# Cross-attention with grouped queries on one core: output weights split during the query projection, reciprocals taken inside attention, last denominator summed on TensorE

## The chip, the cores and the metric

The kernel runs on one core of a Trainium2 chip. The core has TensorE (PE), VectorE (DVE), ScalarE (ACT), GpSimd (POOL) and SyncE (SP), each with its own instruction stream, and 16 DMA engines. The streams are joined only by semaphores that the kernel sets and waits on by hand. The metric is the device time of one execution in microseconds, as the median of several runs.

## The reference, cut to what matters

```python
B, L, S, H, NH, KVH, HD = 4, 1024, 1601, 1024, 32, 8, 32
q, k, v = x @ Wq + bq, ctx @ Wk + bk, ctx @ Wv + bv          # 8 key heads, 4 query heads each
scores = einsum('bkgld,bksd->bkgls', q, k) / sqrt(HD) + mask
attn = softmax(scores, axis=-1)
out = einsum('bkgls,bksd->bkgld', attn, v) @ Wo + bo
x = out + hidden
y = (x - mean(x)) * rsqrt(var(x) + EPS) * gamma + beta
```

All arrays are float32. The mask is all zeros in these inputs; the kernel looks at it and takes a branch without it.

## The kernel before

To keep float32 accuracy in TensorE's fast format, an operand is split in two parts: `hi`, a rounded copy that ACT writes, and `lo`, the rest, which DVE writes as operand minus `hi`. A product is then three matmuls: hi by hi, lo by hi, hi by lo. The program is three blocks one after the other. A block begins only when every engine has ended its stream of the block before, waits for transfers included.

**`project`** makes k and v from 13 chunks of 512 context rows, then q from 8 chunks (NXC) of 512 rows of x. One query chunk is eight groups `g` of 24 matmuls. ACT copies a group's sum to `o_hi` (L308), DVE makes `full` and `o_lo` (L362, L367), POOL stores both (L405). In the last chunk nothing of a next chunk lies beside. SP loads rows and, in query chunks, four mask tiles per chunk into `landing` (L189), which DVE looks through (L346) at odd `g`. POOL waits for its own last store before its stream ends.

**`attend`** runs 64 steps (NSTEP), one for each key head and 512 queries; four steps are a QUAD. The order of TensorE's work in a step is one written string, ORDER: L is a logit tile (13 key tiles by 4 heads), S half a row of scores for the maxima (reduced on DVE, L880), M a product with v of the weights of one key tile, T a transpose of the maxima, P the denominators of the step before. ACT takes the exponents (L933). POOL adds the weight tiles of nine key tiles into `sum_pool` with eight adds (L660); the key tiles of REST = (2, 5, 8, 11) are added to tile 2 by accumulating DMAs that POOL issues (L671), and `merge` (L678) adds that sum to `sum_pool` by one more. P multiplies `sum_pool` with ones (`sum_heads`, L799: four heads, eight instructions in the profile), ACT copies the result to `denom_sb` (L950), SP stores it to `d_dram` (L598). The denominators of step 63 come after everything: the rest of the adds, the merge, `denominators`, the copy, the store. SP's stream in one iteration n of a step is: `load_step` for three steps ahead (q, k, v of 1.5 MB), `store` of the product, `store_sums`, `shift` of the maxima. Near its start it loads 128 of the 1024 rows of Wo, `wo_early`. In the last three steps there is nothing to load.

**`output`** first loads all denominators in two portions (L1048, step 0 to 7 and the rest), takes reciprocals on DVE (L1145), stores them (L1044), and reads them back spread over 32 partitions for each head (`r_in`, L1058); `a_in` holds the products (L1052). DVE multiplies (L1154), ACT and DVE split the result (L1120, L1158). Meanwhile ACT issues the loads of the other seven slices of Wo (L1115) and, after its first `a_hi`, splits them:

```python
            split_hi(0, 0)
            split_weights(range(EARLY, KVH))
            split_hi(0, 1)
```

TensorE (L1103) waits in the first group for each slice of `wo_lo` (L1150), and then runs 1536 matmuls in 16 blocks of 96. Per tile of 128 rows DVE adds x + bo (POOL, L1205), takes the statistics, and normalises; POOL adds beta (L1212) and stores.

Of the kernel before, what the change touches and what calls it, by code (L numbers as in the profile page):

```python
# [20 lines left out]
F32 = mybir.dt.float32  # L21
# [26 lines left out]
EARLY = 1  # L48
# [5 lines left out]
def xattn_program(nc, x, ctx_kv, mask, wq, bq, wk, bk, wv, bv, wo, bo, gamma, beta, out):  # L54
# [10 lines left out]
    r_dram = nc.dram_tensor("reciprocals", [NSTEP, G, LQ], F32, kind="Internal").ap()  # L65

    with ExitStack() as whole:
        ident = whole.enter_context(nc.sbuf_tensor("ident", [P, P], F32))
        mask_size = whole.enter_context(nc.sbuf_tensor("mask_size", [P, MT], F32))
        project(nc, x_flat, ctx_flat, mask_flat, wq, bq, wk, bk, wv, bv, q_dram, k_dram, v_dram, ident, mask_size)  # L70

        wo_early = whole.enter_context(nc.sbuf_tensor("wo_early", [P, EARLY, H], F32))
        attend(nc, mask_flat, q_dram, k_dram, v_dram, a_dram, d_dram, ident, mask_size, wo, wo_early)
        output(nc, x_flat, wo, wo_early, bo, gamma, beta, a_dram, d_dram, r_dram, out_flat)


def project(nc, x_flat, ctx_flat, mask_flat, wq, bq, wk, bk, wv, bv, q_dram, k_dram, v_dram, ident, mask_size):
# [42 lines left out]
    with ExitStack() as held:  # L120
# [11 lines left out]
        bv_row = sb("bv_row", [P, KV])  # L132
# [6 lines left out]
        v_out = [sb(f"v_out{i}", [P, KV]) for i in range(2)]  # L139
# [12 lines left out]
        W_RUNS = (range(KVW), range(KVW, KVW + 3), range(KVW + 3, KVW + 6), range(KVW + 6, len(w_pieces)))  # L152
        w_in = [sem(f"w_in{i}") for i in range(LAND)]
# [23 lines left out]
        def _(sp):  # L177
# [12 lines left out]

            def step(kind, c, par):

                turns = kind == "ctx" and isinstance(c, int) and c == NCC - 1
                following = ("x", 0) if turns else (kind, c + 1)
                for half in range(2):
# [13 lines left out]
            sp.dma_start(bv_row[:], bv.partition_broadcast(P)).then_inc(bias_in, 16)  # L209
            all_chunks(sp, step)  # L210

# [56 lines left out]
        def _(act):  # L268
# [16 lines left out]

            def split_hi(u, t, par):
# [3 lines left out]
            def step(kind, c, par):  # L290
# [4 lines left out]
                for g, beside in enumerate(BESIDE[kind]):  # L295
# [4 lines left out]
                    if kind == "ctx" and isinstance(c, int) and g == 2:  # L300
                        split_weights_hi(W_RUNS[c - NCC + 4])
                    if kind == "x" or g < KG:
# [23 lines left out]
        def _(dve):  # L326
# [14 lines left out]

            def look_through(c, j):
# [6 lines left out]
            def step(kind, c, par):  # L349

                u, n0 = chunk(kind, c), sums(kind, c)
                for g, beside in enumerate(BESIDE[kind]):
# [3 lines left out]
                    if kind == "ctx" and isinstance(c, int) and g == 2:  # L356
                        split_weights_lo(W_RUNS[c - NCC + 4])
                    acc = summed[bank(kind, par, g)]
# [9 lines left out]
                    else:  # L368
# [3 lines left out]
                        nc.vector.tensor_tensor(v_out[j % 2][:], acc[:, 0:KV], bv_row[:], ALU.add).then_inc(sum_read, 1)  # L372
# [13 lines left out]
        def _(pool):  # L386
# [8 lines left out]
            def step(kind, c, par):  # L395
# [12 lines left out]
                if kind == "ctx":  # L408
                    for j in range(XC // P):
                        pool.wait_ge(sum_read, sums(kind, c) + (KG + j + 1 + 4))  # L410
                        pool.dma_start(v_dram[bass.ds(start(c) + j * P, P), :], v_out[j % 2][:]).then_inc(v_stored, 16)  # L411
# [6 lines left out]
def attend(nc, mask_flat, q_dram, k_dram, v_dram, a_dram, d_dram, ident, mask_size, wo, wo_early):  # L418
# [7 lines left out]
    BASES = 2  # L426
    NPOOL = len(POOL) - 1
# [48 lines left out]
    with ExitStack() as held:  # L476
# [7 lines left out]
        q_sb = [sb(f"q_sb{i}", [SHIFT, G, LQ], F32R) for i in range(QB)]  # L484

        k_sb = [sb(f"k_sb{i}", [SHIFT, S], F32R) for i in range(QB)]
# [10 lines left out]
        denom_sb = [sb(f"denom_sb{i}", [P, LQ]) for i in range(2)]  # L497
# [35 lines left out]
        wo_in = sem("wo_early_in")  # L533
        sync_seen = sem("sync_seen")
        mixed_stored = [sem(f"mixed_stored{i}") for i in range(2)]
        denom_stored = [sem(f"denom_stored{i}") for i in range(2)]
# [6 lines left out]
        def _(sp):  # L543
# [50 lines left out]
            def store_sums(step, par):  # L594
# [3 lines left out]
                sp.dma_start(d_dram[bass.ds(step, 1)].rearrange("a h l -> (a h) l"), denom_sb[par][0:P:HD, :]).then_inc(denom_stored[par], 16)  # L598

            def batch(b, first=False, last=False):  # L600
                for lq in range(NB):
                    for n in range(KVH):
# [8 lines left out]
                        elif not last:  # L611
                            load_step(b + 1, 0, ahead % KVH)
# [632 lines left out]
```

## Time and profile before

| | us |
|---|---|
| median of 3 runs | 3967.89 (3964.56 to 3978.52) |
| the profiled execution, its own time | 3971.06 |
| its span | 3969.4 |
| PE busy | 3806.3 (96%) |
| PE weight loads busy | 2407.2 (61%) |
| DVE busy | 2502.5 (63%) |
| ACT busy | 2037.3 (51%) |
| POOL busy | 2905.9 (73%), nine tenths and more in nearly all slices of attention |

Mean granted clock of TensorE 0.963 of full speed. Busy time counts only instructions that compute. In the rows, times count from the start of the span; `[x <-y]` is idle time of the engine before the row and what ended it. PEclk is the granted clock, DMA the mean busy share of 16 engines. `PEld` is a weight load, `SPq`, `POOLq` a sequencer that issues.

### The profile page before, as it was taken

The numbers are of one execution on the slowest core, as the hardware profiler recorded it, in microseconds if no ns is written. First come the engines' busy times: TensorE is split into PE (matmuls) and PEld (weight loads), VectorE is DVE, ScalarE is ACT, GpSimd is POOL, SyncE is SP. The second block draws the span as 40 slices with busy tenths as digits, with TensorE's granted clock in tenths as the row PEclk, the third lists the DMA queues.
The fourth block names the chain that finished last, engine by engine and source line by source line (L and its number), as shares of the span: only waits on it lengthen the run. The fifth ranks groups of instructions, "written<-read, shape, count | busy, mean of one in ns | idle before, by whom it ended". The sixth has DMA issues, their size and how long they took to land. (4 is left out here: it accounts for less than half of the span.)

```text
span 3969.4 us, 66216 instructions
## 1 busy us (share of the span) xinstructions
PE 3806.3 (96%) x20274; PEld 2407.2 (61%) x20274; DVE 2502.5 (63%) x2890; ACT 2037.3 (51%) x3854; POOL 2905.9 (73%) x1108
## 2 busy tenths in 40 slices
PE   8999999799999999999999999999999999967998
PEld 7998888555555555555555555555555555525887
DVE  3334444477767676676777767677676767715666
ACT  2222111056666666666666666666666666641110
POOL 1111111169989899999999999999999999973664
PEclk9999999789999999999999999999999999977999
DMA  5445555547667666766766766666766766655664
GB/s 176 143 139 184 205 200 183 140 94 154 147 132 153 139 141 135 154 137 136 153 144 143 154 135 145 148 145 140 154 137 143 153 135 145 127 139 177 191 196 132
DMA packets 286020, 598.38 MB, mean 151 GB/s; under 512 B 126848, under 2 KB 164096, under 8 KB 252928
## 3 DMA queue, kind: packets, MB, share of 16 engines
q0 software_dynamic: 58368, 339.25, 38.2%
q1 hardware_dynamic: 223056, 245.09, 23.1%
q10 hardware_dynamic: 4272, 9.96, 0.7%
q8 instruction: 175, 2.87, 0.3%
q14 instruction: 149, 1.22, 0.1%
HBM read 236.11 MB, written 88.60 MB: 82 GB/s over the span
## 5 line engine op out<-in xcount | busy, mean ns | idle before, releaser
L880 DVE TENSOR_REDUCE half_max<-score 128x1 f32<-128x800 f32 (+1 forms) x2048 | 1895.0, 986 | 799.5 <-PE score L744 797.3
L933 ACT ACTIVATE weights<-logit 128x512 f32<-128x512 f32 (+1 forms) x3328 | 1736.2, 603 | 855.6 <-PE logit L789 831.4
L660 POOL TENSOR_TENSOR sum_pool<-sum_pool,weights 128x2048 f32<-128x2048 f32 (+1 forms) x448 | 2124.8, 4743 | 40.8 <-ACT weights L933 21.4
L789 PE MATMUL logit<-q_sb,k_sb 98*128 98x512 f32 (+1 forms) x3328 | 1207.4, 420 | 39.8 <-issue 37.2
L744 PE MATMUL score<-k_sb,q_sb 96*128 96x400 f32 (+1 forms) x4096 | 1225.8, 382 | 15.4 <-DMA k_sb<-k_parts 10.6
L744 PEld LDWEIGHTS score<-k_sb,q_sb 96*128 96x128 f32 x4096 | 703.0, 195 | 581.3 <-DVE half_max L880 399.2
L799 PE MATMUL mixed<-weights,v_sb 128*32 128x512 f32 x6656 | 825.0, 610 | 0.7 <-ACT weights L933 0.7
L789 PEld LDWEIGHTS logit<-q_sb,k_sb 98*128 98x128 f32 (+1 forms) x3328 | 618.1, 189 | 280.7 <-issue 151.3
L799 PEld LDWEIGHTS mixed<-weights,v_sb 128*32 128x32 f32 x6656 | 178.8, 110 | 402.2 <-ACT weights L933 223.2
L660 POOL TENSOR_TENSOR sum_pool<-weights 128x2048 f32<-128x2048 f32 x64 | 304.3, 4754 | 114.2 <-ACT weights L933 110.3
L405 POOL DMA_DIRECT2D q_parts<-o_hi x64 | 34.5, 540 | 299.1 <-DMA q_parts<-o_lo 141.6
L1103 PE MATMUL acc<-wo_hi,a_hi 128*128 128x512 f32 x512 | 202.5, 395 | 44.6 <-DVE a_lo L1158 37.7
L308 ACT ACTIVATE o_hi<-summed,bq_scaled 128x512 fp32r<-128x512 f32 x64 | 44.1, 689 | 312.6 <-PE summed L228 312.6
L1103 PE MATMUL acc<-wo_hi,a_lo 128*128 128x512 f32 x512 | 201.6, 394 | 0.0
L1103 PE MATMUL acc<-wo_lo,a_hi 128*128 128x512 f32 x512 | 201.4, 393 | 0.0
L362 DVE TENSOR_SCALAR full<-summed,bq_scaled 128x512 f32<-128x512 f32 x64 | 48.1, 751 | 197.8 <-ACT o_hi L308 197.8
L1212 POOL TENSOR_TENSOR total<-total,beta_row 128x1024 f32<-128x1024 f32 x32 | 102.2, 3193 | 95.5 <-DVE total L1179 95.5
L288 ACT CAST t_hi<-turned 128x512 fp32r<-128x512 f32 x168 | 95.3, 584 | 141.1 <-PE turned L223 140.9
L671 POOL DMA_DIRECT2D weights<-weights x192 | 166.6, 868 | 0.0
L1205 POOL TENSOR_TENSOR total<-total,bo_row 128x1024 f32<-128x1024 f32 x32 | 90.6, 2834 | 80.4 <-DMA total<-in_x 80.1
L411 POOL DMA_DIRECT2D v_rows<-v_out x52 | 28.1, 540 | 162.6 <-DMA v_rows<-v_out 103.8
L333 DVE TENSOR_TENSOR t_lo<-turned,t_hi 128x512 fp32r<-128x512 f32 x168 | 113.0, 685 | 41.8 <-ACT t_hi L288 41.6
(80 smaller groups left out, 2654.4 us busy)
## 6 DMA issues: line engine op xcount, KB each, us to landing
weights<-weights POOLq DMA_DIRECT2D x192, 1024.0 KB, 7.5
sum_pool<-weights POOLq DMA_DIRECT2D x64, 1024.0 KB, 7.3
q_sb<-q_parts SPq DMA_DIRECT2D x192, 256.0 KB, 3.9
k_sb<-k_parts SPq DMA_DIRECT2D x192, 200.1 KB, 6.3
rows<-in_ctx SPq DMA_DIRECT2D x26, 1024.0 KB, 5.2
landing<-in_mask_Bx1xSxS_ff SPq DMA_DIRECT2D x32, 800.5 KB, 5.2
rows<-in_x SPq DMA_DIRECT2D x16, 1024.0 KB, 5.3
q_parts<-o_hi POOLq DMA_DIRECT2D x64, 256.0 KB, 2.3
```

The costliest lines, as they stand in the source:

```text
L288: nc.scalar.copy(t_hi[par][:, t, :], turned[t % 2][:]).then_inc(hi_done, 1)
L333: nc.vector.tensor_tensor(t_lo[par][:, t, :], turned[t % 2][:], t_hi[par][:, t, :].bitcast(F32), ALU.subtract).then_inc(lo_done, 1)
L660: nc.gpsimd.tensor_tensor(sum_pool[s % 2][0:w], first[0:w], weights[buffer(s, st)][0:w], ALU.add).then_inc(pool_added, 1)
L671: pool.dma_start(weights[buffer(s, REST[0])][:], weights[buffer(s, st)][:], accum_op=ALU.add).then_inc(rest_added, 16)
L744: last = nc.tensor.matmul(score[j][:, c, 0:w], q_sb[buf][0:STACK, h, lt * P:(lt + 1) * P], k_sb[buf][0:STACK, start:start + w], start=True ...
L789: last = nc.tensor.matmul(bank[0:w, :], k_sb[s][:, keys], q_sb[s][:, h, :], start=True, stop=not masked, skip_group_check=masked)
L799: last = nc.tensor.matmul(out[h * HD:(h + 1) * HD, :], lhs, rhs[0:w, h, :], start=start, stop=stop)
L880: nc.vector.tensor_reduce(half_max[m // NROW % 2][:, k % G, k // G, j:j + 1], score[j][:, :, 0:HALVES[j][2]], mybir.AxisListType.XY, ALU.m ...
L933: nc.scalar.activation(weights[buffer(s, st)][0:w, h, :], logit[u % BANKS][0:w, :], ACT.Exp).then_inc(exp_done, 1)
L1103: last = nc.tensor.matmul(acc[j * NT + t][:, n, :], a[:, k, cols], w[:, k, out_cols], start=(k == 0 and m == 0), stop=(k == KVH - 1 and m ...
L1205: nc.gpsimd.tensor_tensor(total[r][:], total[r][:], bo_row[:], ALU.add).then_inc(resid_done, 1)
L1212: nc.gpsimd.tensor_tensor(total[r][:], total[r][:], beta_row[:], ALU.add).then_inc(final, 1)
```

## The change

1. Wo is split in `project`, during the last two query chunks: SP loads one slice at a time into `wo_raw` (the buffer of `v_out` and `bv_row`), ACT and DVE split it at g = 1, 3, 5, 7 into the buffers of the k and v weights, and SP stores the eight parts of a chunk to `wo_dram` after its fourth split. The block ends when all sixteen are stored. Ten parts are loaded in the last three steps of attention into the q and k buffers that are then free and one spare; six (3 MB) at the start of `output`.
2. In attention SP loads the denominators of the quad before at n % 4 = 1, DVE takes their reciprocals (128 x 64) in the third step of a quad ahead of its maximum k = 8, and SP stores them at n % 4 = 2. `denom_sb` becomes one buffer. `output` does this only for the last quad, after its first two blocks are ready.
3. In step 63 POOL stops after the key tiles below LATE = 10. TensorE sums what is left itself, five `sum_heads` in one bank: key tiles 10, 11, 12, the tile of the REST sum, and `sum_pool`.

```diff
+        wo_raw = sb("v_store", [P, H])
+        WO_AT = (1, 3, 5, 7)
+            def load_wo(c, t):                         # project, SP
+                k = c * 4 + t
+                if k == 0:
+                    for i in range(2):
+                        sp.wait_ge(v_free[i], NCC * (XC // P // 2) + 1)
+                else:
+                    sp.wait_ge(wo_lo_done, k)
+                sp.dma_start(wo_raw[:], wo[k * P:(k + 1) * P]).then_inc(wo_in, 16)
+            def store_wo(c):
+                sp.wait_ge(wo_lo_done, c * 4 + 4)
+                for t in range(4):
+                    for n, part in enumerate((wo_hi, wo_lo)):
+                        sp.dma_start(wo_dram[2 * (c * 4 + t) + n], part[t].bitcast(F32)).then_inc(wo_stored, 16)
                     for j in range(MPC):
+                        if split:
+                            load_wo(c - NXC + 2, j)
                         load_mask(c, j)
+                    if split:
+                        store_wo(c - NXC + 2)
             all_chunks(sp, step)
+            sp.wait_ge(wo_stored, 16 * 2 * KVH)
+            def split_wo_hi(c, t):                     # ACT, ahead of o_hi of g in WO_AT
+                act.wait_ge(wo_in, (c * 4 + t) * 16 + 16)
+                if c > 0:
+                    act.wait_ge(wo_stored, 16 * KVH)
+                nc.scalar.copy(wo_hi[t], wo_raw[:]).then_inc(wo_hi_done, 1)
+            def split_wo_lo(c, t):                     # DVE, ahead of full of g in WO_AT
+                dve.wait_ge(wo_hi_done, c * 4 + t + 1)
+                nc.vector.tensor_tensor(wo_lo[t], wo_raw[:], wo_hi[t].bitcast(F32), ALU.subtract).then_inc(wo_lo_done, 1)
...
+            def load_wo(j):                            # attend, SP, in iterations 61 to 63
+                sp.wait_ge(logit_done, LOGITS0 + (NSTEP - SLOTS + j) * (ST * G))
+                slots = wo_dram[j * SLOTS:(j + 1) * SLOTS]
+                sp.dma_start(qk_store[j][:, 0:SLOTS * H]..., slots.rearrange("t p n -> p t n")).then_inc(wo_in, 16)
+                if j == 0:
+                    sp.dma_start(wo_spare[:].bitcast(F32), wo_dram[3 * SLOTS]).then_inc(wo_in, 16)
-                            store_sums(step - 1, (n - 1) % 2)
+                            store_sums(step - 1)
+                        if n % QUAD == 1 and not (first and lq == 0 and n < QUAD):
+                            load_sums(quad - 1)
                         if not (final and n == KVH - 1):
                             shift(step + 1, (n + 1) % QB)
+                        if n % QUAD == 2 and not (first and lq == 0 and n < QUAD):
+                            store_reciprocals(quad - 1)
-            sp.dma_start(wo_early[:], wo[0:EARLY * P]...).then_inc(wo_in, 16)
+                    if last and POOL[n + 1] >= LATE:   # POOL, sums()
+                        break
-            merge(NSTEP - 1, QUAD - 1)
+            def last_denominators():                   # PE, after the last product
+                bank, s = logit[SUMS % BANKS], QUAD - 1
+                pe.wait_ge(exp_done, NSTEP * ST * G)
+                for st in range(LATE, ST):
+                    w = min(P, S - st * P)
+                    sum_heads(bank, ones[0:w, :], weights[buffer(s, st)], w, st == LATE, False)
+                pe.wait_ge(rest_added, ...)            # accumulating DMAs of tiles 5 and 8
+                sum_heads(bank, ones[:], weights[buffer(s, REST[0])], P, False, False)
+                pe.wait_ge(pool_added, ...)            # POOL's six adds
+                sum_heads(bank, ones[:], sum_pool[s % 2], P, False, True).then_inc(denom_done, 1)
+            def invert(quad):                          # DVE, at s == 2, k == 8
+                dve.wait_ge(dens_in, quad * 16 + 16)
+                nc.vector.reciprocal(dens[:], dens[:]).then_inc(dens_recip, 1)
...
             for j in range(2):                         # output, SP
                 load_weighted(0, j)
-            store_reciprocals(0)
-            for j in range(2):
                 load_reciprocals(0, j)
+                if j == 0:
+                    sp.dma_start(wo_late[:].bitcast(F32), wo_dram[len(wo_slots):2 * KVH]...).then_inc(wo_late_in, 16)
+            sp.dma_start(dens[:], last_steps(d_dram)).then_inc(dens_in, 16)
             for row, src in ((bo_row, bo), (gamma_row, gamma), (beta_row, beta)):
                 sp.dma_start(row[:], src.partition_broadcast(P)).then_inc(rows_in, 16)
             for j in range(2):
                 load_x(0, j, first=True)
-            store_reciprocals(1)
+            sp.wait_ge(dens_recip, 1)
+            sp.dma_start(last_steps(r_dram), dens[:]).then_inc(dens_out, 16)
+            sp.wait_ge(dens_out, 16)
-                                if t == 0 and n == 0:
-                                    pe.wait_ge(w_lo_done, k + 1)
+                                if t == 0 and n == 0 and k == len(wo_slots) // 2:
+                                    pe.wait_ge(wo_late_in, 16)
             split_hi(0, 0)                             # ACT; DVE likewise
-            split_weights(range(EARLY, KVH))
             split_hi(0, 1)
```

## Rows read from the trace of the kernel before

**Rows 1.** The chain that ended last: start, us, what.
```profile
3559.56 0.35 SPq L1048
3563.17 14.88 DMA reciprocals<-dens
3579.44 7.62 DMA r_in<-reciprocals
3587.08 2.30 DVE a_in L1154
3589.41 1.91 ACT a_hi L1120
3591.34 2.29 DVE a_lo L1158
3593.63 16.63 DVE wo_lo L1150 x7
3610.30 346.34 PE acc L1103 x1515
```
**Rows 2.** Timeline of PE, end of attention: start, us, instructions, idle before.
```profile
3519.49 1.90 PE L799 MATMUL mixed<-weights,v_sb 128*32 128x512 f32 x16
...
3535.73 1.06 PE L799 MATMUL mixed<-weights,v_sb 65*32 65x512 f32 x8 [0.68 <-ACT weights L933]
3554.25 1.94 PE L799 MATMUL logit<-sum_pool,ones 128*32 128x512 f32 x8 [17.45 <-DMA sum_pool<-weights]
3593.90 0.76 PE L1103 MATMUL acc<-wo_hi,a_hi 128*128 128x512 f32 x1 [37.72 <-DVE a_lo L1158]
```
**Rows 3.** Timeline of POOL in step 63.
```profile
3529.64 0.85 POOL L671 DMA_DIRECT2D weights<-weights  x1
3530.24 9.47 POOL L660 TENSOR_TENSOR sum_pool<-sum_pool,weights 128x2048 f32<-128x2048 f32 x2
...
3547.17 0.87 POOL L678 DMA_DIRECT2D sum_pool<-weights  x1 [2.11 <-DMA weights<-weights]
```
**Rows 4.** Timeline of SP, last store of attention.
```profile
3556.94 0.58 SPq L598 DMA_DIRECT2D denominators<-denom_sb  x1
```
**Rows 5.** Windows of 5 us: busy per engine (instructions), PEclk, DMA share, GB/s.
```profile
3570.00:3575.00 5.00, 0.00 (x0) 0.00 (x0) 2.39 (x2) 0.00 (x0) 0.00 (x0) 0.50 1.04 402
...
3580.00:3585.00 5.00, 0.00 (x0) 0.00 (x0) 0.00 (x0) 0.00 (x0) 0.00 (x0) 0.50 0.96 193
...
3610.00:3615.00 5.00, 4.70 (x11) 3.73 (x12) 3.03 (x3) 2.50 (x2) 0.00 (x0) 0.50 0.26 50
3615.00:3620.00 5.00, 5.00 (x21) 4.05 (x21) 2.23 (x2) 0.69 (x1) 0.00 (x0) 0.91 0.00 0
```
**Rows 6.** Timelines of DVE and POOL, end of the query projection.
```profile
743.77 0.69 DVE L367 TENSOR_TENSOR o_lo<-full,o_hi 128x512 fp32r<-128x512 f32 x1
...
750.88 0.54 POOL L405 DMA_DIRECT2D q_parts<-o_lo  x1
755.15 0.12 POOL L644 MEMSET ones<- 128x32 f32 x1 [3.73 <-POOLq L120]
```
**Rows 7.** DMA issues: queue, count, size, median us to landing; last row `a_in` after 3555.
```profile
out<-total POOLq DMA_DIRECT2D x32, 512.0 KB, 2.9
...
q_parts<-o_hi POOLq DMA_DIRECT2D x64, 256.0 KB, 2.3
...
DMA to landing us min/median/max: 5.4/6.7/16.9
```
**Rows 8.** Lines and tiles of DVE: ns min/median/max, or busy us and mean ns.
```profile
L884 DVE TENSOR_REDUCE row_max<-half_max x64: 185/186/189, 807.0 to 3481.9; 128x16 f32<-128x32 f32 x64
...
L1145 DVE RECIPROCAL dens<-dens 128x128 f32<-128x128 f32 x1 | 1.0, 954 | 74.6 <-DMA dens<-denominators 74.6
...
L1150 DVE TENSOR_TENSOR wo_lo<-wo_late,wo_hi x7: 1218/3371/3403, 3593.5 to 3606.9; 128x1024 fp32r<-128x1024 f32 x7
```
**Rows 9.** Timeline of DVE in step 31 or so of attention.
```profile
2110.19 4.59 DVE L880 TENSOR_REDUCE half_max<-score 128x1 f32<-128x804 f32 x5 [1.60 <-PE score L744]
```

More of the change, by code:

```diff
@@ L194, in step @@
                 following = ("x", 0) if turns else (kind, c + 1)
+                split = kind == "x" and isinstance(c, int)
                 for half in range(2):
@@ L481, in sem @@
             return held.enter_context(nc.semaphore(name))
-        q_sb = [sb(f"q_sb{i}", [SHIFT, G, LQ], F32R) for i in range(QB)]
-        k_sb = [sb(f"k_sb{i}", [SHIFT, S], F32R) for i in range(QB)]
+        stores = qk_store + [sb("qk_store3", [P, G * LQ + S], F32R)]
+        q_sb = [store[0:SHIFT, 0:G * LQ].rearrange("p (h l) -> p h l", h=G) for store in stores]
+        k_sb = [store[0:SHIFT, G * LQ:G * LQ + S] for store in stores]
         v_sb = [sb(f"v_sb{i}", [P, ST, HD]) for i in range(QB)]
@@ L678, in merge, with sums @@
                 pool.dma_start(sum_pool[s % 2][:], weights[buffer(s % QUAD, REST[0])][:], accum_op=ALU.add).then_inc(rest_merged, 16)
-            def sums(quad, s, first=False):
+            def sums(quad, s, first=False, last=False):
                 for n in range(NPOOL):
+                    if last and POOL[n + 1] >= LATE:
+                        break
                     for k, st in enumerate(REST):
@@ L712, in queries @@
                             clamp_max(a + 1, range(0, 2) if n == KVH - 2 else range(2, NLT))
-                    sums(a * (KVH // QUAD) + n // QUAD, n % QUAD, first and n == 0)
+                    sums(a * (KVH // QUAD) + n // QUAD, n % QUAD, first and n == 0, final and n == KVH - 1)
             with pool.If(any_mask > 0):
@@ L896, in quad_steps @@
                             copy_lo(quad * QUAD + (s + 1))
+                        if s == 2 and k == 8 and not first:
+                            invert(quad - 1)
                         if not (last and m >= QUAD * NROW):
@@ L948, in copy_denominators @@
                 act.wait_ge(denom_done, quad * QUAD + (s + 3))
-                act.wait_ge(denom_stored[s % 2], quad * 32 + (16 * (s // 2) + 16))
-                nc.scalar.copy(denom_sb[s % 2][:], logit[SUMS % BANKS][:]).then_inc(denom_copied, 1)
+                if not (isinstance(quad, int) and quad * QUAD + s == 0):
+                    act.wait_ge(denom_stored, quad * (16 * QUAD) + 16 * s)
+                nc.scalar.copy(denom_sb[:], logit[SUMS % BANKS][:]).then_inc(denom_copied, 1)
             def quad_steps(quad, first=False, last=False):
@@ L1142, in _ @@
             dve.sem_inc(total_done, RING)
-            for n in range(2):
-                dve.wait_ge(dens_in[n], 16)
-                nc.vector.reciprocal(dens[n][:], dens[n][:]).then_inc(dens_recip, 1)
-            def split_weights(slices):
-                for k in slices:
-                    dve.wait_ge(w_hi_done, k + 1)
-                    nc.vector.tensor_tensor(wo_lo[:, k, :], raw(k), wo_hi[:, k, :].bitcast(F32), ALU.subtract).then_inc(w_lo_done, 1)
             def normalise(i, j):
```

122 lines of the change are left out of this document (69 added, 53 removed).

## The prediction

> **What bounds the kernel now.** I read the table of engines first: TensorE is busy 96% of the span, and a gain inside `project` or `attend` would have to come from its stream. So I looked for where it is not busy. The waits show two gaps of it near one place, and the chain that ended last explains them. The reader should see in the chain that it has no compute between 3559.56 and 3587.08: loading denominators, storing reciprocals (14.88 us), reading them back (7.62 us), then three vector steps of 2.30, 1.91 and 2.29 us, then seven `wo_lo` (16.63 us), and only then 346.34 us of matmuls without a wait [rows 1]. The PE timeline gives the gaps: the last product ends at 3536.79, the last denominators run from 3554.25 to 3556.19 after 17.45 us of idleness, and the first output matmul starts at 3593.90 after 37.72 us more [rows 2]. I then took the POOL timeline for what holds the merge, the windows for rates and clock, and the end of the query projection for the cost of the new work.
>
> All sums are made in the profiled execution, 3971.06 us (span 3969.4), which lies 3.2 us above the median of 3967.89. I subtract the same from both.
>
> **Part 3, the last denominators.** Before: the accumulating DMA of tile 11 starts behind two adds at 3539.7, the merge can start at 3547.17, lands about 7 us later, and TensorE ends at 3556.19 [rows 2, 3]. After: five `sum_heads` follow the last product. Two cost 1.90 us [rows 2], so 0.95 each, 4.75 in all, ending at 3541.5. Their waits are covered: POOL's sixth add is the first of the two that start at 3530.24 and take 9.47, so it ends at 3535.0; the DMA of tile 8 starts at 3529.64 and, with the 7.5 us of the next one (3539.7 to 3547.17), lands at 3537.2, while TensorE asks for it after three sums, at 3539.6 [rows 3]. The cover is 2.4 us; a slower DMA costs what exceeds it. Gain 14.7 us. If TensorE ran at the half clock of the 1.94 us row the five would take 9.7 and the gain be 9.7; it has been busy just before, so I take 14.7. Behind it nothing changes: copy, store and block end took 3559.56 - 3556.19 = 3.4 us [rows 1, 2, 4]. Call the start of `output` T0; it was 3559.56 and is 3544.9 here. The loads of the ten Wo parts take the place of the `load_step` of earlier iterations, 1.5 MB each plus 0.5, and are 35 us old by then.
>
> **Part 2, reciprocals, in output.** T0 to the first matmul was 3593.90 - 3559.56 = 34.3 us. Now `a_in` and four `r_in` are issued at once. Five issues at 0.35 to 0.58 us (the SP rows [rows 1, 4]) are 1.8 to 2.9; I take 2.7, then 7.62 from the last issue to the landing, then 2.30 + 1.91 + 2.29 [rows 1]: 16.8 us. Gain 17.5. The bound above: `a_in` once took 16.9 us to land, when 5.5 MB from two queues were in flight [rows 7]; here 3 MB of Wo parts are issued right behind `r_in`. If they shared bandwidth from the start, `r_in` would land at T0 + 18, the first matmul at T0 + 25, gain 9.5. I take 16.8, since the 7.62 row too had other transfers issued right behind it. Below, nothing faster than 15.
>
> By the Trainium skill, "DMA: Bandwidth & Descriptors", section "Queues, rings and completion order", each DMA engine consumes one queue's descriptors in ring order and takes turns only between queues; all loads here are in SP's queue, while in the trace ACT's queue carried Wo beside `a_in`. That agrees with the 16.9 us, and no row shows the new arrangement; by the rule the sum stays as above, without it the gain is 9.5.
>
> Is the next thing late? The 3 MB at 402 GB/s take 7.8 us, behind 1 MB at that rate (2.6) and 1 MB of spread reads at 193 GB/s (5.4) [rows 5]: landed near T0 + 1.5 + 15.8 + 2 = T0 + 19.3. TensorE needs them after 15 matmuls at half clock (11 in 4.70 us [rows 5]: 6.4 us), at T0 + 23.2. Slack 3.9 us. The second block's inputs, 8 us more: T0 + 27.3, ready after the vector steps at T0 + 34; needed at T0 + 41. The last quad's reciprocals follow, then the third block's load, near T0 + 50, ready T0 + 58; needed at T0 + 63. So no stall, with 4 to 7 us of slack each.
>
> **Part 1, in output.** From its first matmul to its last TensorE took 3593.90 to 3956.64, 362.7 us. Without the waits on `wo_lo` it is the 346.34 of the unbroken run, which already contains about 5 us at the half clock (0.50, then 0.91 [rows 5]), plus the 21 matmuls that ran before 3610.30 at 346.34 / 1515 = 0.229: 351.1. Gain 11.6. The idleness before is 20 us in place of 38, and the granted clock was down in both cases after 17 us, so I keep the slow start.
>
> **Part 1, in project.** TensorE is not touched: the last chunk's groups need a bank back only four groups (22 us) later. What moves is the end of the block. In the last chunk DVE ends `o_lo` of g = 6 at 744.46 [rows 6]; the eighth split costs 1.22 (the `wo_lo` that ran without POOL [rows 8]), so SP stores eight parts of 512 KB from 745.7. A store of 256 KB lands in 2.3 us, one of 512 KB in 2.9 [rows 7]: 1.2 us per 512 KB. 2.9 + 7 x 1.2 = 11.3, plus 1.2 for the last `q_parts` among them: 758.2. The next block began at 755.05 [rows 6]. Cost 3.2 us, all on the path, as everything after waits for the block. Bounds: 0 below (POOL's own stores end it then) and, if writes run at half that rate, 13 above; that it needs 4 MB back to back is what no row shows. The other splits, seven of 1.2 us on DVE and eight of 1 on ACT, lie beside TensorE's 5.6 us groups. The stores of the first four splits make the next wo and mask loads late by some 5 us in the last chunk, where one group's copies are late and catch up.
>
> **Part 2, in attention.** Fifteen reciprocals of 128 x 64 on DVE: half of the 128 x 128 row or less than it, 0.55 to 0.95 us [rows 8]. Ahead of maximum k = 8 it stands within a group of five maxima of 0.92 us, and the next group begins after 1.60 us of idleness [rows 9]; by ORDER TensorE needs k = 8 back only at k = 10, behind a logit and two products. It is hidden up to 1.7 us; cost 0, and by the high price still 0. Two small DMAs per quad on SP come before and after `shift`, which waits for DVE anyway, and their own waits are a step old. POOL and ACT get nothing. Bounds: 0 to 5 us for small delays of POOL, which has about a tenth to spare.
>
> Sum: -14.7 - 17.5 - 11.6 + 3.2 = -40.6. Profiled 3930.5, median 3927.3, say **3928**.
>
> **Rivals.** (a) *The cover is thinner*: stores run at half rate (+10) and `a_in`/`r_in` share with the 3 MB (+8), or the Wo parts or the third block arrive 4 us late. 3928 + 18 = 3946. For it: DMA share is already 1.0 in those windows [rows 5]; against: the three slacks. (b) *The chain is partly not removed*: the sum at the end waits for its DMA and the low clock (+5), the reciprocals' way stays late in `output` so that TensorE stalls once at the third block (+5 to +10): 3940. (c) *Slower: the reciprocal is blocked on DVE.* In `output`, `wo_lo` takes 3371 ns with POOL's adds running and 1218 without [rows 8]. If the reciprocal, too, had to wait for one of POOL's adds of 4.74 us (half of 9.47 [rows 3]), it would take up to 5.3, and TensorE would lose 5.3 - 1.7 = 3.6 us in each of 15 quads, 54 us: 3928 + 54 = 3982. It decides from 4.4 us per reciprocal (40.6 / 15 + 1.7). Against it: the small reduction L884, which reads and writes SBUF in each step with POOL busy nearly throughout, took 185 to 189 ns in all 64 [rows 8].
>
> The rule that bears on (c) is in the Trainium skill, "SBUF — State Buffer", section "Who interferes with whom": an operation with one SBUF input outside the two-port modes does not contend with GpSimd, one with two SBUF inputs does. The L884 and `wo_lo` rows agree with both halves; whether a reciprocal enters a two-port mode is not said there for this instruction, and if it did, (c) would be the outcome.
>
> **Chances.** Forecast 0.68, (a) 0.15, (b) 0.10, (c) 0.04, and 0.03 for a slowing of attention through POOL that eats the gain. What a measurement of this kernel can tell from no change is 0.3%, 12 us, so faster means under 3956. The likeliest case has 3920 to 3937; (a) and (b) end near 3950. I give 3917 to 3952. Faster 0.92, same 0.04, slower 0.04.
>
> **What would show it.** Right: in the new chain, no `wo_lo` and no reciprocals between the attention's end and the first `a_in`; PE idle 20 us between last denominators and first matmul; five `sum_heads` right behind the last product; the output matmuls in one run of 351 us; the attention's first instruction 3 us later. Wrong: PE waits on `wo_late` or `a_lo` in the first four blocks; a first instruction of attention past 762; reciprocals longer than 1.7 us; the distance from 755 to the last product, 2781 us before, longer by more than 3.

## The result and the profile after

Timed side by side, the changed kernel took 3948.64 us (3945.69 to 3967.0) and the kernel before 3975.02 (3953.01 to 4007.95): ratio 0.9945, 95% interval 0.9925 to 0.9965. A second comparison gave 3956.19 against 3975.37, ratio 0.9945 again (0.9925 to 0.9965). By the ratio the gain is 0.55%, 22 us; the medians differ by 26.4 and 19.2. The forecast was 1.0%, 40.6 us: right sign, nearly twice the size.

The profiled execution took 3947.47 us, span 3945.8, 23.6 less than before. Cut at five marks (first instruction of attention on POOL; end of the last product; end of the last denominators; T0; first and last output matmul):

| stage, us | before | after | difference | predicted |
|---|---|---|---|---|
| span start to attention | 755.15 | 767.62 | +12.5 | +3.2 |
| attention to its last product | 2781.6 | 2776.8 | -4.8 | 0 |
| last product to last denominators | 19.4 | 4.5 | -14.9 | -14.7 |
| from there to T0 | 3.4 | 3.0 | -0.3 | 0 |
| T0 to first output matmul | 34.3 | 22.8 | -11.6 | -17.5 |
| output matmuls | 362.7 | 358.3 | -4.4 | -11.6 |

The column before is one execution. Over the six profiles whose kernels have the old end of attention, the last denominators took 19.4 to 21.3 us (mean 20.3), and in the three others with the old `output` unchanged or both its operands moved alike (e6, e8, e11) the output matmuls took 359.3 to 360.4, because the first 21, with their waits, took 14.3 and not 16.4. So part 3 is worth some 1 us more than the table says, and the output matmuls 2 to 3 us less.

The new chain that ended last (start, us, what) answers to [rows 1]. The loading and storing of reciprocals and the seven `wo_lo` are gone, as predicted; the read of `r_in` is not 7.62 us but 13.80, and the matmuls run unbroken, but take 358.32:

```profile
3551.93 0.39 SPq L1133
...
3554.18 13.80 DMA r_in<-reciprocals
3568.00 2.30 DVE a_in L1219
3570.33 1.91 ACT a_hi L1196
3572.26 2.30 DVE a_lo L1223
3574.68 358.32 PE acc L1188 x1536
```

TensorE's timeline, for [rows 2]: four sums (x32) and the fifth (x8) follow the last product without a wait, and end at 3548.88.

```profile
3543.36 1.06 PE L876 MATMUL mixed<-weights,v_sb 65*32 65x512 f32 x8 [0.68 <-ACT weights L1026]
3544.24 3.78 PE L876 MATMUL logit<-weights,ones 128*32 128x512 f32 x32
3547.84 1.04 PE L876 MATMUL logit<-sum_pool,ones 128*32 128x512 f32 x8
3574.68 0.79 PE L1188 MATMUL acc<-qk_store,a_hi 128*128 128x512 f32 x1 [25.80 <-DVE a_lo L1223]
```

The timeline of all engines at the end of the query projection, for [rows 6]. The slice of Wo for g = 1 stands behind the eight stores of the chunk before, and ACT waits 7.67 us for it. The last `o_hi` but one has waited 7.02 us for its buffer, which POOL's stores still hold; the last split ends at 751.81 instead of the predicted 745.7; eight stores follow, and POOL starts attention at 767.62:

```profile
717.26 1.05 ACT L321 CAST wk_hi<-v_store 128x1024 fp32r<-128x1024 f32 x1 [7.67 <-DMA v_store<-in_L_xattn_Wo]
...
748.47 0.69 ACT L347 ACTIVATE o_hi<-summed,bq_scaled 128x512 fp32r<-128x512 f32 x1 [7.02 <-POOLq L452]
748.92 0.54 POOL L450 DMA_DIRECT2D q_parts<-o_hi  x1 [6.64 <-DMA q_parts<-o_lo]
...
750.59 1.22 DVE L383 TENSOR_TENSOR wv_lo<-v_store,wv_hi 128x1024 fp32r<-128x1024 f32 x1
751.83 0.33 SPq L214 DMA_DIRECT2D wo_parts<-wk_hi  x1
...
758.54 1.28 SPq L214 DMA_DIRECT2D wo_parts<-wv_lo  x1
...
767.62 0.12 POOL L720 MEMSET ones<- 128x32 f32 x1 [7.60 <-POOLq L124]
```

The windows there (columns as in [rows 5]) show those stores at full rate, 407 and 413 GB/s:

```profile
755.00:760.00 5.00, 0.00 (x0) 0.00 (x0) 1.14 (x1) 0.00 (x0) 1.05 (x2) 0.50 1.02 407
760.00:765.00 5.00, 0.00 (x0) 0.00 (x0) 0.00 (x0) 0.00 (x0) 0.02 (x1) 0.50 1.02 413
```

The line of the reciprocals in attention (count, busy us, mean ns, idle before): 543 ns each, no idle time.

```profile
L976 DVE RECIPROCAL dens<-dens 128x64 f32<-128x64 f32 x15 | 8.1, 543 | 0.0
```

### The profile page after: what moved, and what is told of

The parts are those of the page before. It is cut to its first block and busy times, and to the rows that moved or that the text cites. A ratio compares the mean times of both kernels' runs of the same rounds, so it can differ in the third digit from the quotient of the medians.

```text
span 3945.8 us, 66424 instructions
## 1 busy us (share of the span) xinstructions
PE 3808.5 (97%) x20306; PEld 2404.1 (61%) x20306; DVE 2496.9 (63%) x2904; ACT 2036.8 (52%) x3854; POOL 2893.7 (73%) x1104
## 5 line engine op out<-in xcount | busy, mean ns | idle before, releaser
L736 POOL TENSOR_TENSOR sum_pool<-sum_pool,weights 128x2048 f32<-128x2048 f32 x446 | 2114.5, 4741 | 41.3 <-ACT weights L1026 22.7
L821 PE MATMUL score<-qk_store 96*128 96x400 f32 (+1 forms) x4096 | 1227.2, 382 | 15.4 <-DMA qk_store<-k_parts 10.5
L866 PE MATMUL logit<-qk_store 98*128 98x512 f32 (+1 forms) x3328 | 1204.4, 420 | 37.8 <-issue 35.6
L821 PEld LDWEIGHTS score<-qk_store 96*128 96x128 f32 x4096 | 702.4, 194 | 580.4 <-DVE half_max L968 401.3
L866 PEld LDWEIGHTS logit<-qk_store 98*128 98x128 f32 (+1 forms) x3328 | 618.2, 188 | 279.0 <-issue 149.7
L1188 PE MATMUL acc<-qk_store,a_hi 128*128 128x512 f32 x576 | 186.8, 396 | 25.8 <-DVE a_lo L1223 25.8
L456 POOL DMA_DIRECT2D v_rows<-v_store x52 | 28.0, 539 | 159.9 <-DMA v_rows<-v_store 111.3
L1188 PEld LDWEIGHTS acc<-qk_store,a_hi 128*128 128x128 f32 x576 | 109.2, 190 | 53.2 <-issue 26.7
L259 PE MATMUL summed<-t_hi,wq_hi 128*128 128x512 f32 x512 | 134.6, 404 | 0.0
```

Of the source, the lines that this page charges most:

```text
L259: last = nc.tensor.matmul(acc, lhs, rhs, start=(n == 0), stop=(n == len(pairs) - 1))
L736: nc.gpsimd.tensor_tensor(sum_pool[s % 2][0:w], first[0:w], weights[buffer(s, st)][0:w], ALU.add).then_inc(pool_added, 1)
L821: last = nc.tensor.matmul(score[j][:, c, 0:w], q_sb[buf][0:STACK, h, lt * P:(lt + 1) * P], k_sb[buf][0:STACK, start:start + w], start=True ...
L866: last = nc.tensor.matmul(bank[0:w, :], k_sb[s][:, keys], q_sb[s][:, h, :], start=True, stop=not masked, skip_group_check=masked)
L1188: last = nc.tensor.matmul(acc[j * NT + t][:, n, :], a[:, k, cols], w[k][:, out_cols], start=(k == 0 and m == 0), stop=(k == KVH - 1 and m ...
```

## The experiments

Kernels given without a ratio were executed once: e1 took 3949.70 us, e2 3949.81, e3 3941.18 and e4 3973.63 (the kernel before beside them 3972.97), e5 3975.18, e6 3955.63, e8 3945.49 and e9 3923.14 (beside them 3968.37), e10 3983.45. These totals carry the chance part of attention (last part of this section), so what follows from a stage is read from that stage's marks.

**Where the output matmuls' 7 us went.** In windows of 100 us in the middle of `output` (columns as in [rows 5]) TensorE is busy throughout at full clock in both kernels, but starts 443 matmuls before and 433 after:

```profile
3700.00:3800.00 100.00, 100.00 (x443) 82.84 (x442) 67.57 (x74) 16.07 (x17) 62.13 (x27) 1.00 0.61 186
```
```profile
3700.00:3800.00 100.00, 100.00 (x433) 80.94 (x432) 62.97 (x73) 12.87 (x15) 61.24 (x27) 1.00 0.67 194
```

No wait and no clock explains that. What differs is the place in SBUF: in the kernel before, the stationary (`a_hi`, `a_lo`) and moving (`wo_hi`, `wo_lo`) buffers all began at 0 modulo 256 bytes of their partition; in the changed one `a` begins at 96, the `qk_store` slots at 0, 32 and 64, `wo_spare` and `wo_late` at 96.

*e1_aligned*, the changed kernel with padded buffers, so that all operands of `output` agree modulo 256:

```diff
-        qk_store = [... (f"qk_store{i}", [P, G * LQ + S], F32R) ...]
+        qk_store = [... (f"qk_store{i}", [P, 3712], F32R) ...]
+        pad = sb("pad", [P, 8])               # project, ahead of v_store
```

> The changed kernel with padding alone: a 32-byte pad ahead of v_store in project, and q and k buffers 3712 elements wide in place of 3649, so that every matmul operand of project and output begins at a multiple of 128 bytes; in the changed kernel the t_hi and t_lo of project and the a_hi, a_lo, wo_late of output begin 32 bytes past a multiple of 64. Theory A (the place of an operand in SBUF sets the pace of a 128x512 matmul): the output matmuls come every 0.227 us as in the kernel before and not every 0.232, so the run of 1536 is 351 us and not 358, and in project the groups of 24 query matmuls go from 5.60 to 5.45 us, which makes project 14 to 20 us shorter. Theory B (the pace comes from something else in the changed output stage, such as DMA traffic or many separate tiles for the weights): both stay, 358 us and 5.60 us. Attention stays at 41.15 us per step in both.

The run fell to 350.20, the predicted 351. The same pad moved `project`'s operands from a distance of 96 bytes to one of 128 and changed nothing there (395 ns mean in place of 396; attention began at 771.72), so that half of the expectation failed. Its chain:

```profile
3585.07 350.20 PE acc L1190 x1536
```

Three one-line changes of the kernel before ask what the place must be: *e4_stationary_32* moves `a` by 32 bytes, *e5_moving_32* moves `wo` by 32 and leaves `a` at 0, *e6_both_64* moves both by 64.

```diff
+        pad = sb("pad", [P, 8])       # e4: ahead of a_hi. e5: ahead of wo_hi, and 56 columns behind wo_lo
+        pad = sb("pad", [P, 16])      # e6: ahead of wo_hi
```

> The kernel before with a 32-byte pad ahead of a_hi in output: the stationary operands a_hi and a_lo begin 32 bytes past a multiple of 64, the moving ones (wo_hi, wo_lo) stay at multiples of 256. If the stationary operand's place counts: the output matmuls go from one every 0.227 us to 0.230 to 0.233, the unbroken run from 346.3 to 351 to 356 us. If only the moving one's counts: 0.227 and 346.3.

> The kernel before with a 32-byte pad ahead of wo_hi in output and 224 bytes behind wo_lo: the moving operands begin 32 bytes past a multiple of 256, the stationary a_hi and a_lo stay at multiples of 256. The stationary ones alone at 32 bytes gave 356.4 us for the unbroken run of 1515 in place of 346.3. Theory R (what counts is the distance between the two operands modulo 256 bytes; it also gives 0.2309 for the changed kernel, where 10 of 24 matmuls have both at 96, and 0.2317 was measured): again 356 us. Theory S (only the stationary operand's own place counts): 346 us.

> The kernel before with 64 bytes ahead of wo_hi in output: moving and stationary operands both begin 64 bytes past a multiple of 256. Theory R (the distance counts): 346 us for the unbroken run. Theory S, or one by which each operand has to begin at a multiple of 256: 350 to 357 us. If multiples of 64 are enough: 346 us as well, which e5 and e8 then have to tell apart.

The rows of the three chains, in that order, against 346.34 in [rows 1]:

```profile
3602.78 356.39 PE acc L1104 x1515
```
```profile
3605.37 355.40 PE acc L1105 x1515
```
```profile
3595.04 346.15 PE acc L1104 x1515
```

Either operand alone off by 32 bytes costs 9 to 10 us in 1515 matmuls (2.6 to 2.9%); both off together cost nothing. For these matmuls the distance between the two operands modulo 256 bytes sets the pace, not where either lies. From start to start, at full clock, they come every 226.7 ns in the kernel before, e1 and e6, and every 233.3 in e4 and e5.

In the changed kernel, where the distances are mixed, the rule is not enough. It has 10 of 24 matmuls at distance 0 (those on `wo_spare` and `wo_late`). If each had its own pace, the loss would be 14/24 of 9.5, 5.6 us, where 7.2 were missing and e1 gave back 8.1. One round of 24 shows why:

```profile
3704.59 0.40 PE L1188 MATMUL acc<-qk_store,a_hi 128*128 128x512 f32 x1
...
3707.84 0.39 PE L1188 MATMUL acc<-wo_spare,a_hi 128*128 128x512 f32 x1
...
3710.16 0.40 PE L1188 MATMUL acc<-qk_store,a_hi 128*128 128x512 f32 x1
```

The 14 on `qk_store` take 3.25 us and the 10 at distance 0 take 2.32: 232 ns each in both. So a matmul at distance 0 isn't at the full pace among others that are not. Why stays open.

*e8_project_256* and, timed, *e11_project_256_timed*: the kernel before had such a distance in its query and key projection (weights at 0, rows of x at 96).

```diff
+        pad = sb("pad", [P, 40])
         bv_row = sb("bv_row", [P, KV])
```

> The kernel before with 160 bytes ahead of bv_row in project: t_hi and t_lo begin at multiples of 512 bytes and the weights at multiples of 256, so the distance between moving and stationary operand is 0 modulo 256; it was 96 before, and 128 in the padded variant of the changed kernel, where the pace stayed at 5.60 us for 24. Theory R: 5.45 us for a group of 24 query matmuls, last project matmul 12 to 20 us earlier than 747.8. Otherwise 5.60 and 747 to 750.

> The kernel before with 160 bytes ahead of bv_row in project, so that the two operands of a matmul of the query and key projection lie at the same place modulo 256 bytes: the same kernel as e8_project_256, timed. Theory R (the distance of the two operands modulo 256 bytes sets the matmul's pace): attention starts 7.5 to 9 us earlier than in the kernel before, and nothing else moves: ratio 0.9975 to 0.9985. The 22.9 us of the single pair would then have been two thirds chance of the attention part. Rival (the pad acts on attention too): ratio 0.9945 or less.

Attention began at 747.56 and 748.40 instead of 755.15 to 757.20 in the four kernels without the pad, 8 us earlier, and 24 query matmuls took 5.44 us instead of 5.60. In the profile's mean a `wq` matmul took 389 ns instead of 396:

```profile
748.40 0.12 POOL L645 MEMSET ones<- 128x32 f32 x1 [3.62 <-POOLq L120]
```
```profile
L229 PE MATMUL summed<-t_hi,wq_lo 128*128 128x512 f32 x512 | 126.6, 389 | 0.0
```

e8's expectation, 12 to 20 us, failed in size: the 8 come from the query projection alone, which begins at 400 us with and without the pad. Before it, what the key matmuls gain the v matmuls lose: these have 256 columns, and with both operands at distance 0 they came every 123.2 ns instead of 121.0. So distance 0 is the faster one for 512 columns only.

The timed ratio is 0.9956 (0.9929 to 0.9983). It shows a gain, and is too wide to tell 8 us from 22: of the expected 0.9975 to 0.9985 it holds most, of the rival's values some. The single pair gave 22.9 us (3945.49 against 3968.37), with attention at its second shortest, 2766.5. In the timed kernel's profile attention took 2785.8, so the marks lend the rival nothing.

**What holds the start of attention.** *e2_spread_stores*: each slice's two stores by themselves, behind the next two loads.

```diff
-            def store_wo(c):                   # eight stores after the fourth split of a chunk
+            def store_wo(k):                   # two stores, behind the next slice and mask tile
+                sp.wait_ge(wo_lo_done, k + 1)
```

> The changed kernel with the split parts of Wo stored one split at a time, each right after the next slice's load, in place of eight stores behind the fourth split. Theory A (the burst of 4 MB is what made project longer: once by holding up the next chunk's weight and mask loads and the q_parts stores, and once at the end): the last split ends near 746 us as planned, only 1 MB of stores follows it, and the first instruction of attention comes at 755 to 757 us and not at 767.6. Theory B (the splits themselves or their loads make project longer): it stays past 762. The rest of the run as in the changed kernel.

It failed: attention began at 771.51, 3.9 later still. Here there is no burst, but 2.3 MB (a slice of Wo, a mask tile, two parts) stand in SP's queue beside each pair of groups. Every second `o_hi` waits 9 us for POOL's stores of `q_parts`, and a pair takes 13.4 us (744.03 to 757.48) where TensorE needs 11.2:

```profile
744.03 0.69 ACT L348 ACTIVATE o_hi<-summed,bq_scaled 128x512 fp32r<-128x512 f32 x1 [8.96 <-POOLq L453]
...
757.48 0.69 ACT L348 ACTIVATE o_hi<-summed,bq_scaled 128x512 fp32r<-128x512 f32 x1 [9.01 <-POOLq L453]
...
771.51 0.12 POOL L721 MEMSET ones<- 128x32 f32 x1 [3.75 <-POOLq L124]
```

So a kernel was made that splits in `project` but stores nothing there (e9, below): attention began at 749.02 and 749.23. Its last project matmul ends at 741.2 to 741.5, attention follows 7.8 us behind, against 19.6 behind in the changed kernel (748.0 to 767.62) and 7.3 in the kernel before (747.8 to 755.15). So it isn't the splits or the loads of Wo, theory B of e2, either; the 8 MB of stores cost 12.

**What holds the first output matmul.** *e3_wo_late_early*: the last six parts (3 MB) are loaded in step 63 into the room of `mask_max`, so nothing of Wo stands behind `r_in`.

```diff
+                if j == 2:                     # attend, SP
+                    sp.wait_ge(score_done, 2 * NROW * NSTEP)
...
+                    sp.dma_start(wo_late[:, 0:6 * H]..., wo_dram[10:16]...).then_inc(wo_in, 16)
...
-                if j == 0:                     # output, SP
-                    sp.dma_start(wo_late[:]..., wo_dram[len(wo_slots):2 * KVH]...)
```

> The changed kernel with the last six Wo parts (3 MB) loaded in step 63 into the room of mask_max, which nobody reads any more by then, so that output begins without that load. Theory A (r_in took 13.8 us to land because the 3 MB behind it in the same queue shared the bandwidth): from the start of output to the first matmul 17 us in place of 22.8, r_in landing 8 to 10 us after its last issue. Theory B (r_in is slow by itself behind a_in, because its spread reads follow 1 MB of other loads): 21 to 23 us as in the changed kernel. Nothing else moves by over 1 us, but for the granted clock in attention.

T0 to the first matmul was 20.19 us, `r_in` 10.93:

```profile
3549.25 10.93 DMA r_in<-reciprocals
```

With the 3 MB behind them five profiles gave 22.75, 20.43, 20.95, 21.65 and 20.56 (mean 21.3), without them 20.19, 20.62 and 20.49 (mean 20.4): the 3 MB cost about 1 us, no more than the five differ among themselves, and not 8. The result lies outside both expectations, 17 and 21 to 23, and nearer to theory B.

Nor was the rest unchanged. In the new place the 3 MB run beside the accumulating DMAs of step 62, whose sum lands late, and TensorE waits for it. No kernel without this load has that wait; e9 has it with 5.37 us and e13 with 2.86. So the move gives 1 us at one place and takes 3 to 6 at another:

```profile
3519.84 1.94 PE L883 MATMUL logit<-sum_pool,ones 128*32 128x512 f32 x8 [5.61 <-DMA sum_pool<-weights]
```

What is left at the start of `output` is `a_in` ahead of `r_in`, both of 1 MB, where the kernel before had loaded `a_in` long since. That it is the order, and not something else in these reads, no run tests. In the windows of e13 (T0 at 3538.84) the first 5 us, start-up included, carry 242 GB/s (`a_in` and the first of the spread read), the next 5 us 174 (the spread read, with all other loads queued behind), together the 2 MB:

```profile
3539.00:3544.00 5.00, 0.00 (x0) 0.00 (x0) 0.00 (x0) 0.00 (x0) 0.00 (x0) 0.51 0.74 242
3544.00:3549.00 5.00, 0.00 (x0) 0.00 (x0) 0.00 (x0) 0.00 (x0) 0.00 (x0) 0.50 0.74 174
```

**The last denominators.** *e10_merge_back*: part 3 undone alone.

```diff
-                last_denominators()
+                pe.wait_ge(exp_done, NSTEP * ST * G)
+                denominators(NSTEP - 1, QUAD - 1)
...
+            merge(NSTEP - 1, QUAD - 1)        # POOL, at the end
```

> The changed kernel with part 3 undone: POOL again adds all of step 63 and merges the REST sum, and TensorE sums sum_pool alone after it. Theory (my step of the prediction holds): the last product's end to the end of TensorE's last denominators goes back from 4.5 us to 19.4 (+14.9), everything behind T0 stays as in the changed kernel (T0 to the first output matmul 20 to 23 us, output run 357 to 360), attention's start 767 to 772. The kernel is then 15 us slower than the changed one, 3961 to 3968 with the random part of attention. Rival (the gain of part 3 was partly only moved: reads of the Wo parts and r_in finish earlier relative to T0 when T0 is later): T0 to the first matmul falls to 17 or less and the loss is 10 or less.

TensorE waited for the merge again, and the stage took 18.6 us instead of 4.3 to 4.6 (+14.2); T0 to the first matmul stayed at 21.65, the run at 358.86. The rival falls. The total, 3983.45, lies above the expected 3961 to 3968, because attention took 2796.2, the longest of all.

```profile
3583.50 1.93 PE L877 MATMUL logit<-sum_pool,ones 128*32 128x512 f32 x8 [16.70 <-DMA sum_pool<-weights]
```

**The findings in one kernel.** *e9_combined*, and timed, *e13_combined_timed*: e3, operands at distance 0 in `output` and in the query projection, and the sixteen parts kept in SBUF through the last two chunks (the second eight in `t_hi[1]` and `t_lo[1]`, free by then) and stored in attention, behind the loads of its first three steps. *e12_changed_timed* is the changed kernel beside it.

```diff
-                nc.scalar.copy(wo_hi[t], wo_raw[:])...
+                nc.scalar.copy(wo_hi[c * 4 + t], wo_raw[:])...      # no wait for stores
...
             load_step(0, 0, 2)                # attend, SP
+            for n, part in enumerate(wo_split):
+                sp.dma_start(wo_dram[n], part.bitcast(F32)).then_inc(wo_stored, 16)
...
+            act.wait_ge(wo_stored, 16 * 2 * KVH)   # ACT, before its first exponents
```

> The changed kernel with four things put together: every matmul operand of project and output at a multiple of 256 bytes; the sixteen parts of Wo kept in SBUF (the second eight in the t buffers that the last chunk leaves free) and stored to memory only in attention's first phase, behind the loads of its first three steps; the last six parts loaded in step 63 into the room of mask_max; the rest as in the changed kernel. Expected against the changed kernel: project's end 7.5 to 10 us behind its last matmul in place of 19.6 (Theory A on the stores' burst; by Theory B, that loads and splits do it, still over 15); the sums for the first step not later, since 8 MB take 20 us of the 45 in which the engines of DMA idle; output run 350.5 us in place of 358.3; from the start of output to its first matmul 20 us. About 3925 to 3932 in all, and 10 to 15 less if theory R holds in project.

> The changed kernel, beside the kernel before on the same chip as e11 and e13. From the parts measured so far: last denominators -14.9, T0 to the first matmul -11.6 to -14, output run -4.4, end of project +12.5 to +16, sum -16 to -22: ratio 0.9945 to 0.996.

> The same kernel as e9_combined, timed. Parts: end of project -6 to -8 against the kernel before (749 against 755 to 757), last denominators -14.9, T0 to first matmul -13.7, output run 350.1 against 362.7, -12.6: sum -47 to -49, ratio 0.9875 to 0.9885 if the attention part is equal; the store of the Wo parts in attention's first steps could cost up to 5 us there, then 0.989 to 0.990. Against the changed kernel 25 to 32 us faster. Rival (what the end of project gave comes back in attention, because the stores slow its loads): 0.993 or more, with the difference between the first instruction of attention and the last product larger by over 10 us than in e12.

It took 3923.55 us (3916.08 to 3940.04), ratio 0.9871 (0.9836 to 0.9906) to the kernel before at 3975.37: 51 us faster than it, and 33 faster than the changed kernel (e12) beside it. e12 itself came out as expected, at the edge of 0.9945 to 0.996. From its timeline and its chain:

```profile
736.64 0.69 ACT L341 ACTIVATE o_hi<-summed,bq_scaled 128x512 fp32r<-128x512 f32 x1 [5.32 <-POOLq L446]
...
749.23 0.12 POOL L723 MEMSET ones<- 128x32 f32 x1 [3.69 <-POOLq L129]
```
```profile
3541.12 11.51 DMA r_in<-reciprocals
...
3559.33 350.18 PE acc L1186 x1536
```

Its attention took 2782.3 (e12: 2793.2), where the rival had over 10 us more. Single profiles differ that much by chance, but the first 150 us of attention, in which the 8 MB are stored (162 GB/s where e12 has 105), tell more: TensorE is busy 130.5 of them, and 130.9 in e12. So what the first stage gave did not come back there. With the wait of 2.86 us this kernel still pays for its early 3 MB.

**Attention.** The middle stage took 2765.6 to 2785.8 us in six profiles with the old attention (mean 2774.2) and 2770.1 to 2796.2 in eight with the new one (mean 2782.9). The difference of 8.7 has a 95% interval of about 10, so the profiles alone don't exclude a cost of reciprocals or sums. The timed runs speak against one: the other stages' means sum to about -18 for the changed kernel, and the time fell by 22, give or take 6 over the two comparisons. Whether the new attention costs a few us stays open; about 0 fits both.

Kernels with the same attention differ by up to 19 us (e8 2766.5, e11 2785.8), and 14 of these 19 are in TensorE's busy time (2711.4 and 2725.7), not in waits. In windows of 50 us (columns as in [rows 5]), the slice with a quad's loop end has TensorE idle 2 to 4 us, and there or behind it the granted clock is lower for a while, by an amount that differs from one to the next. e12_changed_timed, then e3_wo_late_early:

```profile
1500.00:1550.00 50.00, 47.83 (x238) 26.05 (x241) 30.93 (x36) 29.49 (x57) 42.80 (x14) 0.86 0.62 132
1550.00:1600.00 50.00, 49.97 (x282) 27.57 (x278) 36.44 (x42) 34.72 (x68) 48.88 (x16) 1.00 0.70 150
...
2000.00:2050.00 50.00, 46.46 (x228) 25.38 (x227) 29.60 (x34) 28.16 (x55) 41.21 (x14) 0.86 0.58 127
```
```profile
1500.00:1550.00 50.00, 46.34 (x252) 25.81 (x252) 31.82 (x36) 30.18 (x58) 45.03 (x14) 0.93 0.63 135
...
2000.00:2050.00 50.00, 47.83 (x267) 26.26 (x265) 34.83 (x41) 32.97 (x66) 47.63 (x16) 1.00 0.63 135
```

## Why the prediction was right or wrong

**Right.** Part 3 was 14.9 for 14.7, five sums in 4.46 us for 4.75; e10 shows it as a cost of its own. The chain lost the steps it was to lose. Nothing in the first blocks of `output` waited on `wo_late` or `a_lo`: the slacks held. The reciprocal took 543 ns with POOL busy for 92% of attention, far under the 4.4 us from which rival (c) decides. By the Trainium skill, "SBUF — State Buffer", section "Who interferes with whom", an operation with one SBUF input outside the two-port modes doesn't contend with GpSimd; what the page left open for this instruction, the 541 to 544 ns of all fifteen settle.

**Wrong: "Cost 3.2 us", part 1 in project (measured 12.5).** The last split ends 6.1 us late, and from the first store to the start of attention it takes 15.8 us, where the sum had 12.5: 6.1 and 3.3 are the 9.3 that were missing. The stores' price per MB was right, 407 to 413 GB/s. The failed step is "one group's copies are late and catch up". Late they were, by what the prediction names: the `o_hi` of g = 1 started at 718.22 for 714.26 in the kernel before, 4.0 us late, behind a slice of Wo that had stood behind the eight stores. They didn't catch up: the next ones were 6.6, 6.4, 6.0, 4.1, 6.2 and 4.4 us late, though SP stores nothing in that time. Each then waits for POOL's stores, which landed in a median of 4.1 us and not the 2.3 of [rows 7] (about 7 us for the pair issued at 741.21, beside a slice and a mask tile just issued), and SP issues the next slice only after the late split. e13, with the same loads and splits and no stores, keeps TensorE's pace, but two of its `o_hi` already wait for POOL's stores (4.96 and 5.32 us): there was no room to catch up in. Rival (a) named this place with the wrong mechanism, half the store rate. Stores spread (e2, worse) and none (e9, 12 us back) show that the cost comes from storing in this stretch, and not from the burst alone. (The next block began at 755.15, as the row says, and not at 755.05; that makes 3.1 of the 3.2.)

**Wrong: "7.62 from the last issue to the landing", part 2 (measured 10.9 to 13.8).** This row was a read with an empty queue ahead of it. The change puts `a_in` right ahead, and my sum let its 1 MB pass for nothing while it counted it, two paragraphs on, in the slack of the 3 MB. By those same rates, with the 1.5 us for issue and 2 for landing that the prediction gave the 3 MB, 1 MB at 402 GB/s (2.6) and 1 MB at 193 (5.4) land at T0 + 11.5 at the earliest and not at T0 + 10.3; measured were T0 + 13.5 to 16.1 in eight profiles. So the missed term explains 1.2 us of the 5.9, and the rest is that the reads ran slower than those rates (242 and 174 GB/s in e13), for a reason that stays open. The 3 MB behind them, rival (a)'s sharing of 8 us, cost about 1. By the Trainium skill, "DMA: Bandwidth & Descriptors", section "Queues, rings and completion order", a ring is consumed in order, and the 1 us agrees with it; the same rule, applied to what stands ahead, would have given that term.

**Wrong: "351.1", part 1 in output (measured 358.3).** The term that was mis-sized is the run without waits, 346.34 for 1515 matmuls: I took their pace as a property of their shape. It also depends on the operands' places: with these alone changed, e1 gives 350.2. No rival had it, and the `output` before could not show it, since there all four buffers agreed. Its `project` did show a second pace for the same shape, 24 matmuls in 5.60 us or 233 ns each, which the prediction used ("TensorE's 5.6 us groups") and did not ask about (e8).

The three misses are 9.3 + 5.9 + 7.2 = 22.4 us; attention's -4.8 and small items leave the 17.0 between 40.6 and 23.6. About 3946 by the forecast's own base, and 3948.64 as measured, lie inside 3917 to 3952; the second comparison's 3956.19 lies outside, and all miss the 3920 to 3937 of the likeliest case. That 3946 is also rival (a)'s number is luck: its 10 us for stores at half rate and its 8 for sharing with the 3 MB did not occur, and three other misses came to about as much. (The prediction's "near 3950" for (a) and (b) doesn't fit its own 3946 and 3940.)

## What to carry to other kernels

Moving work from an idle stretch into a covered one moves its bytes too: price the stores of neighbours by what they take with the new traffic in flight, not from rows with an empty queue, and look for what they hold (here an `o_hi` buffer and the block's end). A load moved to an earlier place can hold up what it then runs beside, as e3's 3 MB did. A transfer's time is to be taken with what stands ahead of it in its queue. When a buffer is reused for a matmul operand, compare the two operands' start addresses modulo 256 bytes before and after; one pad was worth 8 us here.

## What the runs showed of the hardware

A matmul of 128x128 by 128x512 in the fast format ran at 0.2286 us each (346.34 / 1515) with both operands at the same place modulo 256 bytes, and at 0.2346 to 0.2352 with either 32 bytes off; distances of 96 and 128 bytes, in `project`, cost the same (24 in 5.60 us and not 5.44). Matmuls with 256 columns (v) went the other way, from 121.0 to 123.2 ns from start to start, when their distance went from 96 to 0; I didn't follow this up. Reads that spread one row of 1 KB over 32 partitions ran at 163 to 193 GB/s in windows of 5 us, while plain transfers reached 402 to 413. Each end of the quad loop costs TensorE 2 to 5 us of idleness (35.6 us in 14 waits in the changed kernel), and the granted clock there or behind it is 0.86 to 1.00 as the mean of 50 us. Kernels with the same attention differ by up to 19 us in it, most of it in busy time; that the clock makes this difference is the likely reading, not a tested one.
